# First attention in query blocks of 256, its weights 44 slots behind its maxima, and a block-float feed-forward on three PSUM banks

## The chip, the cores and the metric

One core of a Trainium2 chip runs one launch. The metric is device time in microseconds (us); less is better.

## The reference

The input is x, 2 sequences of 1024 rows of 128 floats.

```python
x = x + attn0(layernorm(x))        # 16 heads of width 8, softmax over all 1024 keys
x = x + ffn0(layernorm(x))         # fp4-quantised gate, up and down, width 352
x = x + encoder(layernorm(x))      # 6 layers: attention with a mask by i & j == 0, LN, gelu FFN of 512
x = x + relu(layernorm(x) @ W1 + b1) @ W2 + b2
```

Quantisation works on blocks of 16 values: the block's largest magnitude over 6 is the scale, each value goes to the nearest of 0, 0.5, 1, 1.5, 2, 3, 4, 6 times it. Activations are quantised before gate and up and again before down.

## The kernel before

**Two passes per attention.** A *half* is one sequence (1024 rows). A half has 4 *units*: unit k is 8 heads (k // 2) against 512 queries (k % 2). The A pass scores with queries on the partitions and takes each query's largest score: PE writes a 128x512 bank of `pA` (4 matmuls side by side on 32 columns of the array each, line 653), DVE reduces it (line 936). 64 such A steps make a unit. `dve_max` (from line 884) joins the unit's maxima, negates them, splits them into three bf16 pieces, and turns them (line 920) into the tile `mt`. SyncE (SP) moves the pieces by DMA into three rows of the stacked queries `QS` (`move_max`, line 1029), so that the B pass's matmul subtracts the maximum by itself.

The B pass scores again with keys on the partitions (line 673, 4 matmuls per 128x512 bank of `pB`), ACT takes the exponential into a ring `PB` of 10 buffers (line 798), and for every 64 keys 4 float32 matmuls of 512 columns multiply by the values and sum in the one bank `pO` (line 688: "AV" below). There are 3 banks `pA`, 2 `pB`, 1 `pO` and 2 `pG`; `pG` serves the small jobs.

**Slots.** Every engine runs the same list of slots, in order (`pe_half`, `act_half`, `dve_half`). A half of the first attention has 256 slots: slot u holds A step u, the B step that is `lead` slots behind (74), the AV whose last B step was 2 slots earlier, and then jobs by name from the table `DENSE_JOBS`, whose entries are (slot, name). Jobs are the projections of the next half (`ht`, `qk`, `split`, `v`), the output path (`oev`, `ot`, `on`, `div`, `aht`, `wo`, `res`), the LayerNorm (`gl`, `gn`) and quantisation (`gr`) in front of the feed-forward, and the feed-forward of the first sequence itself: `gx` transposes, `gg` gate and up of one tile of 128 rows (lines 1276 and following), `gs` silu on ACT, `gm` product on DVE, `gq` quantisation of two tiles on DVE, `gh` transposes, `gd` down. Every queue is in order, so a slot number says only what stands before what.

After the second half come the *drain* slots, in which no A step of the first attention is left: its last 74 B steps, and the first sequence's feed-forward. The second sequence's feed-forward runs among the slots of the second attention, whose table and steps are another path (`sparse`).

**The feed-forward's banks.** A tile's gate and up need two banks. `gate_up` (line 1143) gives the first sequence two pairs, (`pA` 0, 1) and (`pA` 2, `pG` 0), used in turn, and `turn` (line 1144) gives `gh` and `gd` bank `pG` 1. Because `pG` also serves the attention's output, `ot2`, `ot3`, `gg1`, `gg3` and `gh0` wait for each other's readers.

**SP's queue** (`sp_half`) is in order too: moves of maxima, loads of the stacked queries and keys (lines 1005, 1015) and writes of the split queries and keys (lines 1021, 1022). A unit's three moves wait for `dve_max` and for the moves before. PE's first B step of a unit waits for all three.

Of the kernel before, what the change touches and what calls it, by code (L numbers as in the profile page):

```python
# [16 lines left out]
NB = S // P  # L17
# [19 lines left out]
GRID_LOW = (0.25, 0.75, 1.25, 1.75)  # L37

# [46 lines left out]
class AStep:  # L85
# [4 lines left out]
    def __init__(self, k, parts, second, tiles, groups):  # L90
        self.k, self.parts, self.second, self.tiles, self.groups = k, parts, second, tiles, groups
        self.width = parts[0][4]


class BStep:


    def __init__(self, k, parts):
        self.k, self.parts = k, parts
        self.cols = sum(p[3] for p in parts)  # L100


def a_steps(sparse):
    out = []
    for k in range(UNITS):
        x = k % 2
        if not sparse:
            for r in range(NR):
                for gg in range(2):
                    for half in range(2):  # L110
                        out.append(AStep(k, [(gg, x * NR + r, ("half", half), 0, CH)], half, (r,), (gg,)))
            continue
# [33 lines left out]
def b_steps(sparse):  # L146
# [3 lines left out]
    for k in range(UNITS):  # L150
        x = k % 2
        if not sparse:
            sets = [(kt,) for kt in range(NK)]
            pop = dict.fromkeys(range(NK), 0)
        else:
            kts = range(NK) if x == 0 else range(NK // 2)
            pop = {kt: ones_in(kt & 7) for kt in kts}
            sets = [(kt,) for kt in sorted(kts, key=lambda kt: pop[kt]) if pop[kt] < 3]
            sets.append(tuple(kt for kt in kts if pop[kt] == 3))
# [29 lines left out]
class Attn:  # L189
# [3 lines left out]
    def __init__(self, sem, tag, sparse, halves):  # L193
# [3 lines left out]
        self.period, self.lead = (82, 36) if sparse else (256, 74)  # L197
        self.jobs = SPARSE_JOBS if sparse else DENSE_JOBS
        self.end = max(at - (halves - self.owned(name)) * self.period
                       for t in self.jobs.values() for at, name in t) + 1  # L200
        self.a_end = [max(i for i, st in enumerate(self.a) if st.k == k) for k in range(UNITS)]
# [90 lines left out]

    def a_bank(self, half, n):
# [5 lines left out]
    def ring(self, n):  # L299
# [5 lines left out]
PBUF = 10  # L305
ABANKS, BBANKS, OBANKS = 3, 2, 1
# [1346 lines left out]
```

## Time and profile before

| | before |
|---|---|
| runs, us | 1934.43, 1927.29, 1935.47; median 1934.43 |
| the profiled execution, time / span, us | 1923.19 / 1921.4 |
| PE, DVE, ACT busy share | 85%, 73%, 63% |
| mean granted TensorE clock | 0.941 of 2.4 GHz |
| first A step | 44.3 us |
| first B step | 108.2 us |
| last A step's reduction of the first attention ends | 454.7 us |
| last AV of the first attention ends | 528 us |
| first A step of the second attention | 594.6 us |

All times inside the span are microseconds from its start. Busy time of PE is modelled and overlaps itself; the distance between the starts of neighbouring rows tells more. "Idle before <- X" names what ended an engine's wait.

### The profile page before, as it was taken

The page shows a single profiled execution, that of the slowest core. Times are in us where ns is not written, and L with a number is a line of the kernel's source. Part 1 is how long each engine was busy: PE and PEld are TensorE (multiplying, and loading weights), DVE is VectorE, ACT ScalarE, POOL GpSimd, SP SyncE. Part 2 cuts the span into 40 slices and gives each one's busy share as a digit, 9 for nine tenths or more (in the row PEclk, how much of TensorE's full clock was granted, in tenths as well). Part 3 has the DMA queues.
Part 4 walks back from the last instruction along what each step waited for, and adds up shares of the span by engine and source line. Part 5 has one row for each costly group of instructions (what it writes and reads, how often), then busy time and mean ns, then how long its engine had stood idle before and what let it go on. Part 6 is the DMA issues. An engine that isn't in the chain of part 4 may idle for free.

```text
span 1921.4 us, 67094 instructions
## 1 busy us (share of the span) xinstructions
PE 1634.4 (85%) x28905; PEld 909.1 (47%) x28905; DVE 1406.8 (73%) x3351; ACT 1200.9 (63%) x2142; POOL 258.9 (13%) x239
## 2 busy tenths in 40 slices
PE   3899998999856788888989888888889897988896
PEld 1233333233333455655556565555555555655553
DVE  7888888886768767675767768576757676876755
ACT  2157776677831567676766767666766776776652
POOL 2000000000011112020302121121202120301111
PEclk7579999999977899999999999999999999999998
DMA  7022102001031532434242433333333424253000
GB/s 175 1 51 80 39 3 51 3 3 27 5 97 39 142 65 73 100 90 97 54 120 53 129 72 94 74 105 64 79 94 77 111 63 111 53 135 65 7 7 17
DMA packets 153756, 130.83 MB, mean 68 GB/s; under 512 B 65029, under 2 KB 149445, under 8 KB 151445
## 3 DMA queue, kind: packets, MB, share of 16 engines
q1 hardware_dynamic: 136181, 125.75, 26.7%
q8 instruction: 228, 3.74, 0.8%
q10 hardware_dynamic: 17280, 0.79, 0.6%
q14 instruction: 67, 0.55, 0.1%
HBM read 79.25 MB, written 45.88 MB: 65 GB/s over the span
## 4 chain that ended last, share of the span: by engine, by line
PE 39%; DVE 10%; ACT 8%; issue 5%; DMA 4%; ACTq 1%; POOL 0%; SPq 0%; POOLq 0%; DVEq 0%
PE pB L673 8%; PE pO L688 7%; PE pA L653 6%; PE pG L622 5%; PE pG L632 5%; DMA emr<-sce 4%; DVE mx L936 3%; ACT PB L798 3%; PE pG L567 2%; ACT VD L756 2%; ACT HT L711 1%; PE pG L599 1%; DVE bst L475 1%; PE pG L581 1%; PE pG L586 1%
## 5 line engine op out<-in xcount | busy, mean ns | idle before, releaser
L798 ACT ACTIVATE PB<-pB 128x512 f32<-128x512 f32 (+1 forms) x1496 | 838.7, 593 | 436.1 <-PE pB L673 409.5
L936 DVE TENSOR_REDUCE mx<-pA 128x1 f32<-128x512 f32 (+3 forms) x1000 | 635.9, 669 | 114.0 <-PE pA L653 112.8
L673 PE MATMUL pB<-QS,KS 85*32 85x256 bf16 (+3 forms) x11264 | 599.9, 284 | 67.2 <-ACT PB L798 45.1
L653 PE MATMUL pA<-KS,QS 82*32 82x256 bf16 (+2 forms) x8384 | 541.3, 311 | 85.1 <-DVE mx L936 40.1
L688 PE MATMUL pO<-PB,VD 128*32 128x128 f32 (+3 forms) x5632 | 459.0, 399 | 6.7 <-issue 4.9
L673 PEld LDWEIGHTS pB<-QS,KS 85*32 85x32 bf16 x11264 | 261.7, 97 | 342.5 <-ACT PB L798 237.4
L653 PEld LDWEIGHTS pA<-KS,QS 82*32 82x32 bf16 x8384 | 203.8, 97 | 310.2 <-DVE mx L936 112.4
L936 DVE TENSOR_REDUCE mxb<-pA 128x1 f32<-128x512 f32 x304 | 207.0, 681 | 11.0 <-PE pA L653 10.8
L498 POOL TENSOR_TENSOR rstd<-vareps,mhalf 128x4 f32<-128x4 f32 x68 | 69.1, 1017 | 1057.8 <-DVE vareps L484 1056.8
L688 PEld LDWEIGHTS pO<-PB,VD 128*32 128x32 f32 x5632 | 160.3, 111 | 34.7 <-issue 7.5
L622 PE MATMUL pG<-HT,wL 128*128 128x512 f32 x192 | 96.0, 624 | 27.7 <-ACT HT L711 25.2
L840 DVE TENSOR_TENSOR ON<-pG,em 128x288 f32<-128x288 f32 x48 | 20.7, 452 | 120.1 <-ACT em L737 120.0
L632 PE MATMUL pG<-wL,FF 128*128 128x128 f32 x768 | 91.8, 278 | 3.5 <-ACT FF L732 3.5
L632 PEld LDWEIGHTS pG<-wL,FF 128*128 128x128 f32 x768 | 87.5, 192 | 9.5 <-ACT FF L732 9.5
L982 POOL TENSOR_TENSOR VU<-VN 128x512 f32<-128x512 f32 x12 | 15.3, 1276 | 517.8 <-PE pG L586 517.8
L732 ACT ACTIVATE FF<-pG,cL 128x512 f32<-128x512 f32 x96 | 66.0, 687 | 21.2 <-PE pG L622 19.3
L849 DVE TENSOR_TENSOR ON<-ON,pG 128x288 f32<-128x288 f32 x48 | 21.6, 452 | 78.0 <-PE pG L599 77.2
L567 PE MATMUL pG<-HT,wE 128*128 128x512 f32 x112 | 68.7, 705 | 9.0 <-ACT HT L711 8.7
L622 PEld LDWEIGHTS pG<-HT,wL 128*128 128x128 f32 x192 | 33.0, 191 | 76.5 <-issue 45.2
L510 PE MATMUL pG<-ident,N 128*128 128x128 f32 x320 | 54.1, 293 | 16.9 <-DVE N L491 14.7
L491 DVE TENSOR_SCALAR N<-N,mv,rstd 128x128 f32<-128x128 f32 x208 | 57.9, 342 | 12.7 <-POOL rstd L498 12.7
L756 ACT ACTIVATE VD<-VN 64x256 f32<-64x256 f32 x112 | 48.5, 433 | 21.6 <-DVE VN L834 16.0
(186 smaller groups left out, 1526.9 us busy)
## 6 DMA issues: line engine op xcount, KB each, us to landing
scq<-PQ SPq DMA_DIRECT2D x84, 384.0 KB, 3.5
QS<-scq SPq DMA_DIRECT2D x56, 576.0 KB
KS<-sck SPq DMA_DIRECT2D x84, 384.0 KB
sck<-PK SPq DMA_DIRECT2D x28, 384.0 KB, 5.4
wL<-in_wL SPq DMA_DIRECT2D x6, 576.0 KB, 4.7
QS<-mt SPq DMA_DIRECT2D x168, 8.0 KB, 2.1
rE<-in_rE SPq DMA_DIRECT2D x7, 256.0 KB, 12.1
emr<-sce SPq DMA_DIRECT2D x96, 4.0 KB, 1.7
```

The costliest lines, as they stand in the source:

```text
L491: ins = v.tensor_scalar(dst[:, t, :], src[:, t, :], mv[:, t, 0:1], rstd[:, t:t + 1], ALU.subtract, ALU.mult)
L498: g.tensor_tensor(rstd[:, a], vareps[:, a], mhalf[:, a], ALU.pow).then_inc(ln.rs, 1)
L567: pe.matmul(pG[:, bank, :], wE[:, n[1], :], HT[:, c * CH:(c + 1) * CH], start=True, stop=True)\
L622: pe.matmul(pG[:, bank, :], wL[:, D + n[1] * P:D + (n[1] + 1) * P], HT[:, c * CH:(c + 1) * CH], start=True, stop=True).then_inc(F1.filled, 1)
L632: ins = pe.matmul(pG[:, bank, i * P:(i + 1) * P], FF[:, x, k, i * P:(i + 1) * P], wL[:, D + HID + k * D:D + HID + (k + 1) * D], start=(k = ...
L653: ins = pe.matmul(pA[QT * hd:QT * (hd + 1), a.a_bank(half, n), at:at + width], QS[0:R_A, r // NR, head, r % NR * QT:(r % NR + 1) * QT], ro ...
L673: ins = pe.matmul(pB[32 * i:32 * (i + 1), a.b_bank(h, v), at:at + width], KS[0:R_B, head, k0:k0 + 32], allowed(QS[0:R_B, x, head, :], 3, k ...
L688: ins = pe.matmul(allowed(pO[32 * j:32 * j + 32, k % OBANKS, :], 3, kt & 7 if a.sparse else 0), VD[:, col:col + 32], PB[:, a.ring(bank)[0] ...
L732: act.activation(FF[:, x, m, :], pG[:, a.bank[name], :], ACT.Gelu, bias=cL[:, 2 + m:3 + m])\
L756: ins = act.activation(VDv[KT * ab:KT * (ab + 1), half.b, 2 * TC * x + p:2 * TC * (x + 1):2, :, VW * ab:VW * ab + HD], src[:, :, :, ab, :] ...
L798: act.activation(PB[:, pos_, 0:st.cols], pB[:, a.b_bank(h, v), 0:st.cols], ACT.Exp).then_inc(a.b_exped, 1)
L936: v.tensor_reduce(dst[:, gs[0]:gs[-1] + 1, tl[0]:tl[-1] + 1:step], pA[:, a.a_bank(half, n), 0:len(gs) * len(tl) * st.width] .rearrange("p ...
```

## The change

Six things change together, all in the first attention and the first sequence's feed-forward.

1. A unit's queries fall into two blocks (`sub`) of 256. A B step now holds two pairs of heads times 256 queries in its bank in place of one pair times 512: 8 matmuls of 256 columns in place of 4 of 512. Its exponential is still one of 128x512. A unit still has 64 B steps: 32 for block 0, then 32 for block 1.
2. An AV stands behind every second B step and is 4 matmuls of 256 columns; before, behind every fourth, and of 512.
3. `dve_max` runs after 32 A steps, on 16 of the 32 columns; its three transposes (line 920) are as before.
4. `QS` is laid out by block (`QD`), a stack of queries is loaded by two DMAs, and a block's maxima are moved by 12 DMAs (3 pieces times 4 pairs of heads, 16 partitions of 32 values each) in place of a unit's 3 (128 partitions of 32).
5. `lead` is 44 in place of 74.
6. The first sequence's feed-forward has one gate and up pair (`pA` 0, 1) and turns in `pA` 2, so it no longer touches `pG`; the waits between `pG`'s users go, and `DENSE_JOBS` is a new table. POOL clears `mp` once at the start.

```diff
-        self.period, self.lead = (82, 36) if sparse else (256, 74)
+        self.period, self.lead = (82, 36) if sparse else (256, 44)
...
+            for sub in range(SUBS):
+                for kt in range(NK):
+                    parts = []
+                    for j0 in range(0, NJ, SUBS):
+                        bank = [(kt, j0 + i, i * SQ, SQ) for i in range(SUBS)]
+                        parts += [(kt, j, len(steps), o, w) for kt, j, o, w in bank]
+                        steps.append(BStep(k, bank, sub))
+                    bundles.append((k, len(steps) - 1, parts))
...
-                    if n == a.a_end[st.k]:
-                        dve_max(v, a, half, st.k)
+                    if n == a.a_end[st.k][st.sub]:
+                        dve_max(v, a, half, st.k, st.sub)
...
-            sp.dma_start(QS[0:R_PAIR, x, hs, :], q[:, hs, x * CH:(x + 1) * CH])\
-                .then_inc((a.stack, a.stack_x1)[x][s], 16)
+            for u in range(SUBS):
+                at = x * CH + u * SQ
+                sp.dma_start(QD[0:R_PAIR, x, u, hs, :], q[:, hs, at:at + SQ]).then_inc(there, 16)
...
+                for hd in range(NQ):
+                    p0 = QT * hd + QT // SUBS * sub
+                    head = SH * s + 2 * hd
+                    sp.dma_start(QD[R_A + i:R_A + i + 1, x, sub, head:head + 2, :].rearrange("p h t -> p (h t)"),
+                                 mt[p0:p0 + QT // SUBS, x, i, :]).then_inc(a.m_loaded, 16)
...
-        gate_up = [[(pA[:, 0, :], pA[:, 1, :]), (pA[:, 2, :], pG[:, 0, :])], [(pB[:, 0, :], pB[:, 1, :])]]
-        turn = [pG[:, 1, :], pO[:, 0, :]]
+        gate_up = [[(pA[:, 0, :], pA[:, 1, :])], [(pB[:, 0, :], pB[:, 1, :])]]
+        turn = [pA[:, 2, :], pO[:, 0, :]]
...
-                if not a.sparse and half.off == 1 and x == 2:
-                    pe.wait_ge(gu_done, 2)
-                if not a.sparse and half.off == 1 and x == 3:
-                    pe.wait_ge(gu_done, FT)
-                    pe.wait_ge(dn_added, FU)
...
-                elif b == 0 and n == 1:
-                    pe.wait_ge(A0.ot_read, UNITS + 1)
-                if b == 0 and n == 3:
-                    pe.wait_ge(A0.res, CB + 1)
...
-                if b == 0 and n == 0:
-                    pe.wait_ge(A0.aht_ready, CB + 1)
```

The table of jobs moves names between slots. Its ACT part in the drain (slots counted from the first half's start, so that 512 is the first drain slot):

```diff
-    "act": [(9, "gw0"), (512, "gx0"), (513, "gx1"), (515, "gs0"), (515, "gs1"), (269, "oev2"), (272, "on2"), (276, "aht0"),
-          (539, "gs2"), (539, "gs3"), (541, "gh0"), (545, "gh1"), (547, "gs4"), (-219, "ht0"), (549, "gs5"),
+    "act": [(512, "gx0"), (512, "gx1"), (9, "gw0"), (522, "gs0"), (534, "gs1"), (534, "gs2"), (537, "gs3"),
+          (540, "gh0"), (541, "gh1"), (541, "gs4"), (545, "gs5"), (548, "gh2"), (548, "gs6"), (549, "gh3"),
```

What it does to the queues, at the places of which the prediction speaks. First PE in the middle of a half, where A and B steps alternate (A is `pA`, B is `pB`, AV is `pO`). Before:

```order
L688 MATMUL pO<-PB,VD 32x512 x4
L653 MATMUL pA<-KS,QS 32x512 x4
L673 MATMUL pB<-QS,KS 32x512 x4
L653 MATMUL pA<-KS,QS 32x512 x4
L673 MATMUL pB<-QS,KS 32x512 x4
L653 MATMUL pA<-KS,QS 32x512 x4
L673 MATMUL pB<-QS,KS 32x512 x4
L653 MATMUL pA<-KS,QS 32x512 x4
L673 MATMUL pB<-QS,KS 32x512 x4
L688 MATMUL pO<-PB,VD 32x512 x4
```

Changed:

```order
L712 MATMUL pO<-PB,VD 32x256 x4
L675 MATMUL pA<-KS,QS 32x512 x4
L695 MATMUL pB<-QS,KS 32x256 x8
L675 MATMUL pA<-KS,QS 32x512 x4
L695 MATMUL pB<-QS,KS 32x256 x8
L712 MATMUL pO<-PB,VD 32x256 x4
```

Half an AV stands after two slots where a whole one stood after four.

Then SP from the first stack loads on. Before:

```order
L1015 DMA KS<-sck 24x8192 x3
L1005 DMA QS<-scq 72x8x512
L1029 DMA QS<-mt 1x128x32 x3
L1005 DMA QS<-scq 72x8x512
L1015 DMA KS<-sck 24x8192 x3
```

Changed:

```order
L1055 DMA KS<-sck 24x8192 x3
L1046 DMA QS<-scq 72x8x256 x2
L1088 DMA QS<-mt 1x16x32 x24
L1046 DMA QS<-scq 72x8x256 x2
L1055 DMA KS<-sck 24x8192 x3
```

The 24 moves are 12 for each block of a unit; the rest of the order is the same.

Last ACT in the drain, from the feed-forward's transposed input (`HT<-pA`) on; `PB<-pB` is a B step's exponential, the other `pA` rows are silu. Before:

```order
L1310 ACTIVATE HT<-pA 128x512
L798 ACTIVATE PB<-pB 128x512 x2
L1316 ACT_TABLE_LOAD
L1316 ACTIVATE FF<-pA 128x352
L1316 ACTIVATE x<-pA 128x352
L798 ACT_TABLE_LOAD
L798 ACTIVATE PB<-pB 128x512 x10
```

Changed:

```order
L1360 ACTIVATE HT<-pA 128x512 x2
L823 ACTIVATE PB<-pB 128x512 x10
L1366 ACT_TABLE_LOAD
L1366 ACTIVATE FF<-pA 128x352
L823 ACT_TABLE_LOAD
L823 ACTIVATE PB<-pB 128x512 x12
L1366 ACT_TABLE_LOAD
L1366 ACTIVATE x<-pA 128x352
L1366 ACTIVATE FF<-pA 128x352
L823 ACT_TABLE_LOAD
```

The first tile's silu stands 10 exponentials behind the transposed input, the second's another 12 behind; before, both stood 2 behind it. Between here and the first sequence's last silu there are 14 table loads in place of 10.

## Rows read from the trace of the kernel before

**Rows 1.** Windows, all engines: busy us (instructions), granted TensorE clock, DMA share, GB/s.
```profile
44.30:77.00 32.70, 32.65 (x211) 8.81 (x215) 28.46 (x47) 2.67 (x6) 0.00 (x0) 0.50 0.05 11
77.00:107.00 30.00, 22.05 (x126) 7.62 (x129) 23.50 (x45) 6.07 (x12) 0.00 (x0) 0.56 0.06 14
107.00:117.00 10.00, 9.50 (x80) 2.42 (x76) 7.04 (x11) 5.62 (x11) 0.00 (x0) 0.50 0.78 153
120.00:250.00 130.00, 125.40 (x1748) 41.03 (x1744) 111.22 (x198) 96.39 (x179) 0.00 (x0) 1.00 0.16 45
250.00:360.00 110.00, 98.80 (x1312) 34.01 (x1301) 98.51 (x196) 72.70 (x133) 2.03 (x2) 0.98 0.11 24
360.00:454.70 94.70, 91.46 (x1268) 30.08 (x1272) 80.49 (x136) 70.00 (x131) 0.00 (x0) 1.00 0.01 2
454.70:548.00 93.30, 70.98 (x608) 30.96 (x600) 60.45 (x139) 64.64 (x118) 9.45 (x9) 0.96 0.09 18
548.00:594.60 46.60, 29.93 (x102) 19.37 (x102) 33.41 (x61) 17.08 (x37) 0.00 (x0) 0.75 0.49 131
```

**Rows 2.** Windows of line 653 (maxima's scores) alone: four matmuls are one step.
```profile
44.30:77.00 32.70, 26.82 (x192) 5.23 (x196) 0.50 0.05 11
77.00:120.00 43.00, 19.96 (x160) 4.22 (x159) 0.57 0.27 56
120.00:250.00 130.00, 67.94 (x696) 18.44 (x692) 1.00 0.16 45
250.00:360.00 110.00, 50.54 (x512) 13.75 (x508) 0.98 0.11 24
360.00:454.70 94.70, 48.92 (x500) 13.37 (x500) 1.00 0.01 2
```

**Rows 3.** Timeline, a clean stretch, PE then ACT: start us, us, instruction, idle before.
```profile
201.45 0.40 PE L653 MATMUL pA<-KS,QS 82*32 82x512 bf16 x4 [0.72 <-DVE mx L936]
201.90 1.03 PE L688 MATMUL pO<-PB,VD 128*32 128x512 f32 x8
202.98 0.39 PE L673 MATMUL pB<-QS,KS 85*32 85x512 bf16 x4
...
204.78 1.03 PE L688 MATMUL pO<-PB,VD 128*32 128x512 f32 x8
...
203.42 2.19 ACT L798 ACTIVATE PB<-pB 128x512 f32<-128x512 f32 x4 [0.70 <-PE pB L673]
```

**Rows 4.** Timeline of DVE, seven reductions with nothing between.
```profile
601.99 4.34 DVE L936 TENSOR_REDUCE mx<-pA 128x1 f32<-128x512 f32 x7
```

**Rows 5.** Timeline of PE in the second attention, B steps of 256 columns.
```profile
651.28 0.39 PE L673 MATMUL pB<-QS,KS 85*32 85x256 bf16 x8
651.50 0.39 PE L653 MATMUL pA<-KS,QS 82*32 82x512 bf16 x4
```

**Rows 6.** Timeline at the end of a unit's maxima.
```profile
197.68 0.39 PE L653 MATMUL pA<-KS,QS 82*32 82x512 bf16 x4
...
200.85 1.76 SPq L1029 DMA_DIRECT2D QS<-mt  x3
```

**Rows 7.** Lines 1029 and 1043: DMA issue, ns min/median/max, and landing.
```profile
L1029 SPq DMA_DIRECT2D QS<-mt x168: 468/594/1531, 101.4 to 1817.1; - x168
...
DMA to landing us min/median/max: 1.9/2.1/10.4
...
L1043 SPq DMA_DIRECT2D emr<-sce x96: 303/432/1997, 620.6 to 1790.3; - x96
```

**Rows 8.** Groups of ACT, 454.7 to 528 us: count, busy, mean ns, idle before.
```profile
L798 ACT ACTIVATE PB<-pB 128x512 f32<-128x512 f32 x74 | 40.8, 600 | 9.7 <-PE pB L673 9.4
L1316 ACT ACT_TABLE_LOAD x5 | 6.4, 1283 | 0.1
```

**Rows 9.** Timeline of PE: one tile's gate and up.
```profile
461.10 1.45 PE L1276 MATMUL pA<-wF,HT 128*128 128x352 f32 x4
```

**Rows 10.** Page, groups: weight loads of line 673, count, busy, mean ns, idle.
```profile
L673 PEld LDWEIGHTS pB<-QS,KS 85*32 85x32 bf16 x11264 | 261.7, 97 | 342.5 <-ACT PB L798 237.4
```

More of the change, by code:

```diff
@@ L291, in owned, with moved @@
         return self.halves - 1
+    def moved(self, k, sub):
+        block = 16 * NP * (NQ if self.subs > 1 else 1)
+        return block * (self.subs * k + sub + 1)
     def a_bank(self, half, n):
@@ L305 @@
 PBUF = 10
+SUBS = 2
+SQ = CH // SUBS
 ABANKS, BBANKS, OBANKS = 3, 2, 1
@@ L687, in pe_half @@
                             col = ((h.b * NK + kt) * (H // 2) + NJ * (k // 2) + j) * PW
-                            ins = pe.matmul(allowed(pO[32 * j:32 * j + 32, k % OBANKS, :], 3, kt & 7 if a.sparse else 0),
+                            out, q0 = pO[32 * j:32 * j + 32, k % OBANKS, :], SQ * a.b[bank].sub
+                            ins = pe.matmul(allowed(out, 3, kt & 7) if a.sparse else out[:, q0:q0 + SQ],
                                             VD[:, col:col + 32], PB[:, a.ring(bank)[0], at:at + width],
-                                            start=(kt == 0), stop=(i + 1 == a.av_end[k]), tile_position=(0, 32 * j),
+                                            start=(kt == 0), stop=(i + 1 == a.av_end[k] or not a.sparse and kt == NK - 1),
+                                            tile_position=(0, 32 * j),
                                             skip_group_check=True)
@@ L882, in dve_job, with dve_max @@
                 ln_norm(v, ln2, N, N, c, half, ln_in)
-        def dve_max(v, a, half, k):
-            x, kb = k % 2, k % 2
-            m, e = mx[:, kb, :], emx[:, kb, :]
+        def dve_max(v, a, half, k, sub):
+            x, kb, z = k % 2, k % 2, a.subs * k + sub
+            cols = slice(sub * MC // a.subs, (sub + 1) * MC // a.subs)
+            m, e = mx[:, kb, cols], emx[:, kb, :]
+            hi, mid, lo = (mp[:, i, cols] for i in range(NP))
+            res = mres[:, cols]
             def mxw(i):
-                half.wait(v, a.mx, MXN * k + i, MXN * UNITS)
-            half.wait(v, a.a_reduced, a.a_end[k] + 1, a.na)
+                half.wait(v, a.mx, MXN * z + i, a.nmx)
+            half.wait(v, a.a_reduced, a.a_end[k][sub] + 1, a.na)
             if a.sparse:
@@ L931, in dve_half @@
                     if n == a.a_first[st.k]:
-                        half.wait(v, a.mx, MXN * (st.k - 1), MXN * UNITS)
+                        half.wait(v, a.mx, MXN * a.subs * (st.k - 1), a.nmx)
                     gs, tl = st.groups, st.tiles
                     step = tl[1] - tl[0] if len(tl) > 1 else 1
-                    dst = (mxb if st.second else mx)[:, kb, :].rearrange("p (g r) -> p g r", g=2)
+                    dst = (mxb if st.second else mx)[:, kb, st.sub * MC // a.subs:(st.sub + 1) * MC // a.subs]\
+                        .rearrange("p (g r) -> p g r", g=2)
+                    tl = [r % (NR // a.subs) for r in tl]
                     v.tensor_reduce(dst[:, gs[0]:gs[-1] + 1, tl[0]:tl[-1] + 1:step],
@@ L1024, in move_max @@
         def move_max(sp, a, half, k):
[L1025 to L1030 removed]
+            for sub in range(a.subs):
+                move_rows(sp, a, half, k, sub)
             if a.sparse and k < UNITS // 2:
```

93 lines of the change are left out of this document (60 added, 33 removed), and 34 rows, old and new, of the table DENSE_JOBS.

## The prediction

> **What bounds the kernel now.** I read the windows by stage first. The first attention with its fill and drain takes the span up to 548 us; the 46.6 us after it [rows 1] and the 1327 us from 594.6 us to the end hold no line whose instructions or order change, so the time must move before 548 us. Line 653's own windows turn stages into slots [rows 2]: 48 steps by 77 us and 40 more by 120 us (12 of these with B steps), 174 to 250 us, 128 to 360 us, 125 to 454.7 us. That is 0.75 us a slot in the two clean stretches (299 slots in 224.7 us) and 0.86 us in the middle, where the first sequence's LayerNorm and quantisation keep DVE at 98.5 of 110 us [rows 1].
>
> The timeline shows what a clean slot waits for [rows 3]. AV starts at 201.90 and again at 204.78: 2.88 us for four slots. The work between is 8 A and B steps, 0.22 us apart, and one AV of 0.86 us (202.76 less 201.90, the row before 202.98 by 0.22): 2.60 us. The missing 0.28 us are PE's waits for ACT: while PE spends 0.86 us in one AV, ACT runs dry (it was idle 0.70 us before 203.42), and then two `pB` banks are too few to catch up at 0.55 us an exponential. PE is the bound, but its work comes in lumps. At a unit's end a second wait stands: DVE is away in `dve_max`, and PE stood 0.72 us for it at 201.45. DVE needs 0.60 us a slot (seven reductions in 4.34 us, the last still running 0.68) [rows 4].
>
> The drain from 454.7 to 548 us is a third case: DVE is busy 60.5 of 93.3 us, ACT 64.6, PE 71 [rows 1], and each waits for the others in the chain gate and up, silu, product, quantisation.
>
> **The steady slots: AV in halves.** Two slots now hold 4 steps of 0.22 and half an AV, 0.43: 1.30 us. One bank's loop is score to exponential 0.44 us (202.98 to 203.42), exponential 0.60, back to PE 0.05: 1.09 us for two banks, and two exponentials take 1.10. Both fit into 1.30, so ACT's wait goes: 0.65 in place of 0.72 us a slot, -0.07. Against it, `dve_max` comes twice as often. Of the 3.2 us from a unit's last A step at 197.68 to the first move at 200.85 [rows 6] some 1.4 are the score, a short queue and the 0.68 us reduction; the other 1.7 to 1.8 are `dve_max`, five small operations and three transposes, which I cost the same at half the width; with 0.60 + 1.7/32 = 0.65 us a slot DVE is now as full as PE, and the 0.7 us wait comes once in 32 slots in place of 64: +0.015. Net -0.055 us over 299 clean slots is -16 us. In the 128 crowded slots DVE rules, and I take -3 us. Together **-19 us**. Ends: nothing gained, or all of 0.75 - 0.65 over the 299 slots, -30 us.
>
> Does a matmul of 256 columns cost half of one of 512? The second attention has them: eight of 256 at 651.28, and the next group starts at 651.50 [rows 5], 0.22 us like four of 512. I cost the doubled count at nothing; it is hidden because four column groups of the array run side by side. The Trainium skill speaks against this: "TensorE: Matmul & The Clock Gate", section "Back-to-back issue gap", gives a stream of weight load and matmul pairs some 81 ns a matmul at 128 columns and 131 ns at 512. By a straight line between those two figures, an estimate, eight pairs of 256 would take 0.76 us against 0.52 for four of 512. The measured 0.22 decides, since those groups run the very same shape.
>
> **The moves of maxima.** Before, three moves were issued in 1.76 us from 200.85 [rows 6], 3.2 us after the unit's last A step started at 197.68, and landed 2.1 us after issue [rows 7]; 3.2 + 2 x 0.59 + 2.1 = 6.5 us, against 11 slots of 0.72 and the wait, 8.9. So there was room, and no B step waits for them to speak of. Now 12 stand in SP's queue: 3.2 + 11d + 2.1 us. PE reaches the B step after 13 slots of 0.65, one step and the 0.7 to 1.0 us wait for DVE: 9.7 us. The deadline is met for d up to 0.40 us. No row shows a move of 16 partitions. The nearest are the old move, 0.594 us with 128 partitions, and line 1043's with 32 partitions, 0.432 us, and 0.303 at least [rows 7]. I take 0.43, from the row nearest in size: arrival at 10.0 us, PE waits 0.3 us a block. Of the 13 blocks between 120 us and the last A step 9 lie in clean slots: **+3 us**. Ends: 0.30 us, no wait; 0.594, arrival at 11.8 and 2.1 us a block, +19 us and about +2 in the crowded ones. Behind a waiting PE stand A steps too, so nothing hides this.
>
> The Q stacks' second DMAs add about 0.3 us of issue before the first A step; the clearing of `mp` on POOL is done long before DVE asks for it. I count both as nothing.
>
> **The fill.** B steps now start at slot 44, about 74.5 us, not at 108.2. The 42 slots up to 120 us took 45.5 us with 12 B steps; now all carry one. At full clock PE needs 42 x 0.65 = 27 us and some 5 for the projections. The clock was at 1.2 GHz in nearly all of 44 to 107 us and still for 10 us after the B steps came, with PE busy 9.5 of 10 us, and at 2.4 GHz from then on [rows 1]. If it rises again 10 us after PE fills up, that adds 5 us: 37 us. DVE needs 42 x 0.60, 7 for splits, 1 for values, 1.7 for `dve_max`: 35. Both fit into 45.5 us, but they wait for each other and for ACT. I take **+2 us**. Ends: -5 us; and +19 us if the clock stays low throughout (42 x 1.30 + 10 = 65 us).
>
> **The drain.** 30 of 74 B steps leave it, 16.4 us of ACT at 0.548 us. They were cover, not bound: ACT had 40.8 us of exponentials and 10 table loads of 1.28 us [rows 8]. What bounds the drain next is the chain through DVE, whose 60.5 us of work stay. New idle time stands at its head: the first tile's silu comes behind 10 exponentials (5.5 us), gate and up of 1.45 us [rows 9] and a table load; the second behind 12 more with two loads. DVE has 4.6 us of other work before the first and 0.5 between, so it idles some 14 us. One pair of banks in place of two sets each tile's gate and up behind the tile before; from the third tile on DVE has 3 to 4 us of quantising between two products, enough for 1.45 + 0.5 us and mostly for the four added table loads (5.1 us on ACT). I leave 10 us for this, for the second sequence's output path (`aht1`, `wo1`), and the last down product. 60.5 + 14 + 10 = 84.5 against 93.3: **-9 us**. What it gives up are waits for `pG` and the tail from the last AV at 528 us to 548 us, when the second sequence's path ran alone; with B steps done about 50 us after the last A step it runs beside quantisation. Ends: -19 us (no idle but the head's) and +5 us.
>
> **Sum.** -19 + 3 + 2 - 9 = -23 us. The profiled execution took 1923.2 us (span 1921.4 and 1.8 around it); it would be 1900. The median of the runs, 1934.4, lies 11.2 us above it, and I carry the difference over: **1911 us**.
>
> **Rivals.**
> *The moves come late* (slower). Place: PE's first B step of each block; SP's queue decides, not PE. Each 0.1 us of d above 0.43 costs 1.1 us a block, about 14 us in 13 blocks. The gain is gone at d near 0.6; from 0.70 us on the change is slower by over 0.5%. At 0.75 us: 9 x 3.85 + 4 x 2.3 = 44 us, so -19 + 44 + 2 - 9 = +18, **1952 us**. For it: the one row of this very kind of move is 0.594, its maximum 1.5. Against: every transfer with fewer partitions is cheaper to issue. Chance 0.13.
> *The ends give nothing back.* The one pair of banks makes the drain as long as before less 2 us, and the fill pays 12 us at low clock: -19 + 3 + 12 - 2 = -6, **1928 us**. For it: ACT, PE and DVE wait in turn, in order, and the table loads grow. Against: the 33 us that DVE idles in the old drain. Chance 0.25.
> *Short matmuls cost more.* If the weight loads of line 673 did not hide, each 97 ns on average [rows 10], four more a slot would be 0.39 us over 468 slots, +182 us: **about 2090 us**. Nothing in [rows 5] shows it. Chance 0.02. (It is the mechanism that the Trainium skill's rule above would have.)
> The forecast keeps 0.60.
>
> **Numbers.** A measurement of this kernel tells about 0.5%, 9.7 us, from no change. Faster by more (under 1924.8): the forecast's 0.60 and 0.07 of the second rival, 0.67. Within 0.5%: the rest of the second rival and 0.01 of slow moves, 0.19. Slower: 0.12 and 0.02, 0.14. Range: downward steady slots at -27, drain at -16 and no wait for moves give 1892; upward the old move's 0.594 us (+18) alone gives 1929, with part of the fill's low clock 1940. I give 1891 to 1940.
>
> **What the next profile shows if this is right.** AV rows 1.30 to 1.35 us apart and PE's waits for `PB` nearly gone; 0.69 us a slot between 120 us and the last A step, which ends near 441 us; 12 issues of about 0.43 us, and waits of PE for `QS<-mt` of a few tenths; the clock at 2.4 GHz from about 85 us; DVE's last quantisation in front of the second attention's projections about 85 us after the last A step. It is wrong if PE waits over 1 us a block for the moves, if the clean slots stay above 0.72 us, or if the drain lasts 93 us again.

## The result, and the profile after

| us | before | after |
|---|---|---|
| median of the runs on this chip | 1930.86 (4 runs, 1923.33 to 1935.47) | 1968.51 (4 runs, 1946.25 to 1979.82) |
| ratio | | 1.0119, interval 1.0065 to 1.0173 |
| the profiled execution, time / span | 1923.19 / 1921.4 | 1946.25 / 1944.5 |
| mean granted clock | 0.941 | 0.933 |
| first A step | 44.3 | 46.2 |
| last A step's reduction ends | 454.7 | 484.5 |
| first A step of the second attention | 594.6 | 616.7 |

The change is slower, by 1.2% (0.7 to 1.7); 1911 us was forecast. The ratio leaves out the two executions of the change that took over 1.5% longer than its quickest, so it is smaller than the quotient of the medians (1.0195). The profiled execution is the quickest of the four. The two profiled executions differ by 23.1 us: +1.8 up to the first A step, +28 from there to the last reduction (438.3 in place of 410.4), -7.7 from there to the second attention (132.2 in place of 139.9), +1.0 after it. So the whole loss lies in fill and steady slots, where I had expected a gain of 14.

The waits of PE between 40 and 520 us, longest in total first (total, times, longest):

```profile
PE pB L695 <- DMA QS<-mt: 24.6, 12, 2.6
PE pA L675 <- DMA KS<-sck: 20.7, 1, 20.7
PE pA L675 <- DVE mx L971: 10.1, 14, 1.5
PE pA L675 <- DVE mxb L971: 7.4, 6, 2.6
PE pB L695 <- ACT PB L823: 7.1, 11, 1.6
```

The first of them is new: the first B step of a block (line 695, formerly 673) waits for the moves of its maxima, 2.05 us on average, in 12 blocks. This is the change's timeline at such a place, first PE from the block's last A step on, then the last two operations of `dve_max` and SP:

```profile
230.29 0.40 PE L675 MATMUL pA<-KS,QS 82*32 82x512 bf16 x4
...
238.80 0.39 PE L695 MATMUL pB<-QS,KS 85*32 85x256 bf16 x8
239.24 0.39 PE L695 MATMUL pB<-QS,KS 85*32 85x256 bf16 x8
...
239.89 0.39 PE L675 MATMUL pA<-KS,QS 82*32 82x512 bf16 x4
242.40 0.40 PE L695 MATMUL pB<-QS,KS 85*32 85x256 bf16 x8 [2.12 <-DMA QS<-mt]
...
232.53 0.17 DVE L944 TENSOR_TENSOR mp<-mres,mp 128x16 bf16<-128x16 f32 x1
232.74 0.40 DVE L953 STREAM_TRANSPOSE mt<-mp 128x32 bf16<-128x32 bf16 x3
...
233.16 8.03 SPq L1088 DMA_DIRECT2D QS<-mt  x12
```

SP issues twelve moves one behind another in 8.03 us, 0.67 us each, starting 0.02 us after the transposes end. The last lands at 242.4, 12.1 us after the block's last A step started at 230.29 (10.0 were forecast). PE had come at 240.28, 10.0 us after it (9.7 forecast). Over the steady slots an issue of 16 partitions took as long as the old one of 128 [rows 7]:

```profile
L1088 SPq DMA_DIRECT2D QS<-mt x159: 502/589/1992, 100.7 to 459.6; - x159
...
DMA to landing us min/median/max: 1.6/1.8/3.3
```

The windows by stage, in the columns of [rows 1]:

```profile
44.00:77.00 33.00, 29.33 (x191) 7.68 (x191) 28.78 (x53) 2.07 (x5) 0.00 (x0) 0.50 0.10 19
77.00:120.00 43.00, 40.55 (x740) 22.70 (x742) 36.92 (x68) 32.10 (x61) 0.00 (x0) 0.92 0.18 38
120.00:250.00 130.00, 113.72 (x2532) 72.73 (x2524) 105.55 (x198) 88.69 (x163) 0.00 (x0) 0.95 0.21 52
250.00:360.00 110.00, 95.63 (x1928) 58.67 (x1924) 95.13 (x198) 68.04 (x124) 2.03 (x2) 0.89 0.12 24
360.00:460.00 100.00, 88.80 (x1936) 56.02 (x1932) 82.82 (x156) 67.49 (x124) 0.00 (x0) 0.93 0.02 3
```

From 120 to 460 us PE is idle for 42 of 340 us (19 before), and the granted clock, 0.98 to 1.00 before, is 0.89 to 0.95. Five windows of 5 us around the wait that ends at 190.15 show how the two hang together:

```profile
180.00:185.00 5.00, 4.34 (x108) 2.75 (x104) 4.86 (x14) 3.58 (x7) 0.00 (x0) 1.00 0.03 6
185.00:190.00 5.00, 3.26 (x76) 1.82 (x68) 3.98 (x7) 2.85 (x6) 0.00 (x0) 1.00 0.03 5
190.00:195.00 5.00, 4.85 (x56) 2.53 (x60) 1.41 (x3) 2.17 (x4) 0.00 (x0) 0.51 0.00 0
195.00:200.00 5.00, 5.00 (x108) 3.06 (x104) 3.76 (x6) 3.25 (x7) 0.00 (x0) 0.81 0.01 3
200.00:205.00 5.00, 5.00 (x128) 3.56 (x121) 4.88 (x9) 4.09 (x8) 0.00 (x0) 1.00 0.02 5
```

PE stands 1.89 us (until 190.15), and then runs at 1.2 GHz for the next window and part of the one behind it (means 0.51 and 0.81): 56 matmuls in 5 us that otherwise hold 128. The clock fell in this way behind five of the nine waits for moves of about 1.9 us or more between 120 and 460 us, those that end at 163.0, 190.2, 294.5, 388.3 and 415.4:

```profile
163.00:169.60 6.60, 6.59 (x88) 3.61 (x92) 3.15 (x5) 2.98 (x5) 0.00 (x0) 0.50 1.03 338
190.20:196.80 6.60, 6.60 (x76) 3.40 (x80) 2.19 (x4) 2.77 (x5) 0.00 (x0) 0.50 0.00 0
296.00:302.60 6.60, 6.38 (x76) 3.11 (x68) 3.46 (x5) 3.77 (x7) 0.00 (x0) 0.50 0.01 2
388.20:394.80 6.60, 6.54 (x88) 3.71 (x92) 3.09 (x5) 2.98 (x5) 0.00 (x0) 0.50 0.01 2
415.50:422.10 6.60, 6.60 (x76) 3.38 (x80) 2.21 (x4) 2.77 (x5) 0.00 (x0) 0.50 0.01 2
```

Not every wait does it: after the 2.12 us at 242.40 the clock stayed at 1.00. Where no such wait stands the halves of AV do what was forecast: in a clean stretch (205.19, 206.50, 207.81) AV starts are 1.31 us apart, which is 0.655 us a slot.

My theory after reading: the moves come too late because SP needs 0.6 us for each, and a standing PE loses clock besides. Rivals: the new drain or its job order costs time in the steady part; the short matmuls and halves pay less than thought; only the waits count.

### The profile page after: what moved, and what is told of

It is laid out like the page before. It is cut to its first block, busy times and chain, and to the rows that moved or that the text cites. A ratio compares the mean times of both kernels' runs of the same rounds, so it can differ in the third digit from the quotient of the medians.

```text
span 1944.5 us, 73514 instructions
## 1 busy us (share of the span) xinstructions
PE 1630.8 (84%) x31977; PEld 1017.2 (52%) x31977; DVE 1421.7 (73%) x3415; ACT 1209.0 (62%) x2146; POOL 259.1 (13%) x240
## 4 chain that ended last, share of the span: by engine, by line
PE 40%; DVE 10%; ACT 8%; issue 5%; DMA 4%; ACTq 1%; POOL 0%; POOLq 0%; DVEq 0%
PE pB L695 8%; PE pO L712 7%; PE pA L675 6%; PE pG L637 5%; PE pG L647 5%; DMA emr<-sce 4%; ACT PB L823 3%; DVE mx L971 3%; PE pG L587 2%; ACT VD L781 2%; ACT HT L736 1%; PE pG L614 1%; DVE bst L495 1%; PE pG L601 1%; PE pG L606 1%
## 5 line engine op out<-in xcount | busy, mean ns | idle before, releaser
L695 PE MATMUL pB<-QS,KS 85*32 85x256 bf16 (+3 forms) x13312 | 611.6, 268 | 86.4 <-ACT PB L823 48.9
L675 PE MATMUL pA<-KS,QS 82*32 82x256 bf16 (+2 forms) x8384 | 547.8, 312 | 84.0 <-DVE mx L971 43.9
L712 PE MATMUL pO<-PB,VD 128*32 128x256 f32 (+3 forms) x6656 | 490.4, 367 | 9.2 <-issue 6.4
L695 PEld LDWEIGHTS pB<-QS,KS 85*32 85x32 bf16 x13312 | 319.1, 98 | 311.5 <-ACT PB L823 123.4
L712 PEld LDWEIGHTS pO<-PB,VD 128*32 128x32 f32 x6656 | 192.8, 112 | 26.6 <-issue 9.5
L637 PE MATMUL pG<-HT,wL 128*128 128x512 f32 x192 | 97.0, 630 | 27.7 <-ACT HT L736 25.2
L647 PEld LDWEIGHTS pG<-wL,FF 128*128 128x128 f32 x768 | 87.5, 192 | 9.4 <-ACT FF L757 9.4
L530 PEld LDWEIGHTS pG<-ident,N 128*128 128x128 f32 x320 | 36.6, 148 | 49.3 <-issue 21.6
```

The costliest lines, as they stand in the source:

```text
L530: ins = pe.transpose(pG[:, bank, i * P:(i + 1) * P], src[:, TC * c + i, :], ident[:, :])
L637: pe.matmul(pG[:, bank, :], wL[:, D + n[1] * P:D + (n[1] + 1) * P], HT[:, c * CH:(c + 1) * CH], start=True, stop=True).then_inc(F1.filled, 1)
L647: ins = pe.matmul(pG[:, bank, i * P:(i + 1) * P], FF[:, x, k, i * P:(i + 1) * P], wL[:, D + HID + k * D:D + HID + (k + 1) * D], start=(k = ...
L675: ins = pe.matmul(pA[QT * hd:QT * (hd + 1), a.a_bank(half, n), at:at + width], query_tile(a, r, head), row[:, keys * CH:(keys + 1) * CH] i ...
L695: ins = pe.matmul(pB[32 * i:32 * (i + 1), a.b_bank(h, v), at:at + width], KS[0:R_B, head, k0:k0 + 32], allowed(QS[0:R_B, x, head, :], 3, k ...
L712: ins = pe.matmul(allowed(out, 3, kt & 7) if a.sparse else out[:, q0:q0 + SQ], VD[:, col:col + 32], PB[:, a.ring(bank)[0], at:at + width], ...
```

## The experiments

Ten kernels ran, two of them twice, each beside the kernel before, whose medians there were 1925.6 to 1927.6 us. "Steady" below is the distance from the first A step to the start of the last reduction, "drain" from there to the second attention's first A step; both come from the one profiled execution. Before: 409.7 and 140.6. After: 437.6 and 132.9.

### Three moves a block

The maxima of the two blocks stand in alternate columns of `mx`, so the transposes put a block's maxima on every second partition, and one DMA per piece moves them.

```diff
-            cols = slice(sub * MC // a.subs, (sub + 1) * MC // a.subs)
+            cols = slice(sub, MC, a.subs)
...
-                for hd in range(NQ):
-                    p0 = QT * hd + QT // SUBS * sub
-                    head = SH * s + 2 * hd
-                    sp.dma_start(QD[R_A + i:R_A + i + 1, x, sub, head:head + 2, :].rearrange("p h t -> p (h t)"),
-                                 mt[p0:p0 + QT // SUBS, x, i, :]).then_inc(a.m_loaded, 16)
+                sp.dma_start(QD[R_A + i:R_A + i + 1, x, sub, SH * s:SH * (s + 1), :].rearrange("p h t -> p (h t)"),
+                             mt[sub::SUBS, x, i, :]).then_inc(a.m_loaded, 16)
```

(The reductions write to the same alternate columns, and the semaphore's count per block is smaller.) Expected: 

> The changed kernel, but the maxima of the two blocks stand in alternate columns, so that a block goes out in 3 moves of 64 partitions in place of 12 of 16; nothing else differs. Theory (the moves come late, and PE's stall also brings its clock down): 3 issues of 0.59 us, arrival at 3.2 + 1.2 + 2.1 = 6.5 us against the deadline of 9.7; PE's waits for QS<-mt fall from some 2 us a block to under 0.3, the clock stays at 2.4 GHz between 120 us and the last A step, which ends near 445 us and not at 484; about 1905 us. Rival 1 (only the waits count, the clock falls for another reason): waits gone, 25 us gained, about 1921, windows still at 0.89 to 0.95. Rival 2 (halves of AV and short matmuls do not pay): no more than 5 us gained, above 1940.

Measured: 1906.63 us median of 4 (1900.45 to 1921.16), ratio to before 0.9891 (0.9831 to 0.9952). Steady 405.4, drain 130.4. PE's waits in 40 to 520 us:

```profile
PE pA L675 <- DMA KS<-sck: 23.3, 1, 23.3
PE pB L695 <- ACT PB L823: 11.6, 14, 2.0
PE pA L675 <- DVE mx L970: 10.6, 15, 1.5
PE pA L675 <- DVE mxb L970: 6.7, 5, 2.6
```

and its issues of moves in the steady slots:

```profile
L1084 SPq DMA_DIRECT2D QS<-mt x42: 468/597/1469, 103.0 to 429.2; - x42
```

What follows: the waits for `QS<-mt` are gone, and with them 32.2 us of the steady part (27.7 in this kernel's second profile, further down), against 24.6 us that PE had waited. The median is 62 us under the change's; from profile to profile, where the change's execution was its quickest, 35 us. The clock is back at 1.00 from 120 to 250 us and from 360 us on, but not between 250 and 360 us (0.89). An issue still takes 0.6 us; only their number has changed. The moves made the change slow, and it is now faster than the kernel before. Most of that gain lies in the drain, 10.2 us shorter than before; the steady part is shorter by 4.3 us.

### Six moves a block

Against the version with three moves (the semaphore's count changes with it):

```diff
-                sp.dma_start(QD[R_A + i:R_A + i + 1, x, sub, SH * s:SH * (s + 1), :].rearrange("p h t -> p (h t)"),
-                             mt[sub::SUBS, x, i, :]).then_inc(a.m_loaded, 16)
+                for g in range(2):
+                    head = SH * s + 4 * g
+                    sp.dma_start(QD[R_A + i:R_A + i + 1, x, sub, head:head + 4, :].rearrange("p h t -> p (h t)"),
+                                 mt[64 * g + sub:64 * (g + 1):SUBS, x, i, :]).then_inc(a.m_loaded, 16)
```

Expected: 

> moves3 with 6 moves a block (32 partitions each) in place of 3. By issues of 0.59 us whatever their size, the last lands at 3.2 + 6 x 0.59 + 2.1 = 8.8 us against the 9.7 us at which PE comes: no waits for QS<-mt to speak of, steady part as in moves3, about 1900 to 1915 us. If an issue's price grew with small partitions, waits of about 1 us a block would show, and 1920 us.

Measured: 1912.47 us median of 8, ratio 0.9929 (0.9897 to 0.9961). Steady 396.2. No wait for `QS<-mt` stands among PE's. What follows: twice as many issues cost nothing while they fit before the deadline. The price begins at a threshold, it is no slope from the first move on.

### The moves alone, in the kernel before

The kernel before, whose unit's three moves are cut into twelve by pairs of heads; lead 74, one block a unit. The second attention keeps its three.

```diff
             for i in range(NP):
...
-                sp.dma_start(QS[R_A + i:R_A + i + 1, x, SH * s:SH * (s + 1), :].rearrange("p h t -> p (h t)"),
-                             mt[:, x, i, :]).then_inc(a.m_loaded, 16)
+                for hd in range(NQ):
+                    head = SH * s + 2 * hd
+                    sp.dma_start(QS[R_A + i:R_A + i + 1, x, head:head + 2, :].rearrange("p h t -> p (h t)"),
+                                 mt[QT * hd:QT * (hd + 1), x, i, :]).then_inc(a.m_loaded, 16)
```

Expected: 

> The kernel before, but each unit's 3 moves of maxima in 12 of 32 partitions (512 columns each a head pair); lead 74, one block a unit, drain as before. Theory: 12 x 0.59 us of issue puts arrival at 11.8 to 12.0 us against 8.9 of room, so PE waits some 3 us at each of 7 units, and the clock falls behind each: +21 us of waits and some 15 of clock, 1955 to 1970 us. Rival 1 (waits alone): +21, 1945 to 1952. Rival 2 (an issue costs less with fewer partitions, as I forecast, 0.43): +7 at most, under 1942.

Measured: 1959.37 us median of 4 (1958.38 to 1960.36), ratio 1.0158 (1.0134 to 1.0183). The wait and the issues of line 1036:

```profile
PE pB L674 <- DMA QS<-mt: 21.2, 7, 3.4
...
L1036 SPq DMA_DIRECT2D QS<-mt x84: 502/591/1619, 105.9 to 447.7; - x84
```

and its windows:

```profile
120.00:250.00 130.00, 120.31 (x1608) 38.85 (x1604) 101.70 (x176) 88.54 (x164) 0.00 (x0) 0.95 0.22 56
250.00:360.00 110.00, 95.62 (x1196) 32.76 (x1188) 87.40 (x174) 66.84 (x123) 2.02 (x2) 0.92 0.11 23
```

What follows: the model of the deadline holds on the kernel before, too. It gave 2.9 us a unit, and 21.2 / 7 = 3.0 were measured. The steady part grew by 32.4 us (442.1 less 409.7) for 21.2 us of waits, and the medians by 31.7 us. The other 11 go with the clock at 0.92 to 0.95 in place of 0.98 to 1.00: worked out from these means, an estimate, PE spent some 41 us of 120 to 460 us at 1.2 GHz in place of 4. So a late transfer cost about one and a half times its wait. The rival that only the waits count falls here; that the clock is all of the rest is the natural reading, and no kernel changes the clock alone.

### More slots between maxima and weights

The change with its twelve moves, `lead` 52 in place of 44, and the first attention's output path 8 slots later:

```diff
-        self.period, self.lead = (82, 36) if sparse else (256, 44)
+        self.period, self.lead = (82, 36) if sparse else (256, 52)
```

Expected: 

> The changed kernel with its 12 moves a block, but B steps 52 slots behind the A steps in place of 44, and the first attention's output path shifted by the same 8 slots. Theory (late moves): 8 more slots are 5.2 us more room against 2.2 us of wait, so the waits for QS<-mt go as with 3 moves and the clock stays up; 8 more B steps in the drain cost 0 to 4 us: 1900 to 1915 us. Rival 1 (only waits count): about 1922. Rival 2 (the steady slots do not pay): above 1940.

Measured: 1917.26 us median of 5, ratio 0.9935 (0.99 to 0.997). Steady 401.8, drain 139.5, no wait for `QS<-mt` in PE's list. What follows: the other remedy works as well, so at twelve DMAs it is the room that decides. It costs 7 us in the drain.

The same with three moves, leads 48 and 52. Expected, lead 48: 

> 3 moves a block as in moves3 and B steps 48 slots behind. Theory: no move wait was left with 3 moves, so more lead gives nothing in the steady part; the output path shifted by 4 slots moves DVE's div1 behind less of the quantisation; the drain holds 4 more B steps: within 6 us of moves3, 1900 to 1912. Rival (room still short, waits counted elsewhere): 10 us or more below moves3.

Expected, lead 52: 

> 3 moves a block and B steps 52 slots behind. Against lead52 (12 moves) it tells what the 12 issues still cost when PE has 5.2 us more room: theory nothing but disturbance of SP, equal to lead52 within 5 us, and its steady part equal to moves3's; drain 4 to 9 us longer than moves3's: 1908 to 1918. Rival (12 moves cost even when hidden): 10 us below lead52, near 1900.

Measured: lead 48 1907.62 us median of 10 (0.9902, 0.9866 to 0.9939), steady 403.3, drain 132.4; lead 52 1913.82 us median of 10 (0.9935, 0.9903 to 0.9968), steady 402.9, drain 139.5. Twelve or three moves at lead 52 are the same within the spread: issues that end before PE comes cost nothing to be seen. Slots beyond 48 only lengthen the drain.

### The drain alone, and one pair of banks alone

First the new drain in a kernel with one block a unit, lead 74 and three moves a unit (`SUBS` 1; the output path shifted by 30 slots, which is my own placing).

```diff
-        self.period, self.lead = (82, 36) if sparse else (256, 44)
+        self.period, self.lead = (82, 36) if sparse else (256, 74)
...
-SUBS = 2
+SUBS = 1
```

Expected: 

> The changed kernel with one block a unit, lead 74 and 3 moves a unit, so the stacks, steps and moves of the kernel before, with the new drain (one pair of banks, new job order; the first attention's output path shifted by 30 slots). It shows the drain and its table alone. Forecast of my steps: the drain from the last A step to the last quantisation some 3 to 8 us shorter, steady slots as before; 1920 to 1932 us. Rival (the new table costs time outside the drain, or one pair of banks lengthens it): above 1940 us.

Measured: 1935.71 us median of 10, ratio 1.0044 (1.0019 to 1.0069). One of the ten took 3879.9 us; it left no profile, is not in the ratio, and what happened in it stays unknown. Steady 406.1, drain 155.2, which is 14.6 us longer than before and no gain at all. So the drain's gain in the change came from the shorter lead (with the output path that moved along with it), and something in the new drain takes back more than I had allowed. The next kernel says what: the kernel before with one pair of banks for gate and up.

```diff
-        gate_up = [[(pA[:, 0, :], pA[:, 1, :]), (pA[:, 2, :], pG[:, 0, :])], [(pB[:, 0, :], pB[:, 1, :])]]
-        turn = [pG[:, 1, :], pO[:, 0, :]]
+        gate_up = [[(pA[:, 0, :], pA[:, 1, :])], [(pB[:, 0, :], pB[:, 1, :])]]
+        turn = [pA[:, 2, :], pO[:, 0, :]]
...
-         ... (557, "gg7"), (-210, "qk00"), (558, "gd1"), (-208, "qk01"), ...
+         ... (-210, "qk00"), (558, "gd1"), (559, "gg7"), (-208, "qk01"), ...
```

(`gs7` on ACT moves with `gg7`; the waits that guarded `pG` go.) Expected: 

> The kernel before with one thing of the change: gate and up of the first sequence in one pair of banks in place of two, the turn in pA's third bank (in the job order the last gate and up goes behind the second down product, which one pair demands). Forecast of my steps: each gate and up (1.45 us) waits for the product before it but is mostly hidden behind 3 to 4 us of quantising: 0 to +10 us, 1925 to 1940. Rival (the drain of one_block, 155 us from the last A step to the second attention in place of 141, comes from the one pair): about +14 us, 1940 or more.

Measured: 1944.41 us median of 4 (1943.17 to 1950.03), ratio 1.0119 (1.008 to 1.0157). Steady as before (408.5), drain 160.2. From the waits of all engines from 445 to 570 us, those of the feed-forward:

```profile
DVE FF L1339 <- ACT FF L1307: 12.7, 3, 4.9
DVE X L1363 <- PE pA L1290: 11.9, 3, 5.0
DVE FF L1339 <- ACT x L1307: 10.4, 4, 4.0
PE pA L1267 <- DVE FF L1339: 9.3, 5, 2.6
```

What follows: with one pair, gate and up (line 1267) wait 9.3 us for the products, and DVE's products (line 1339) 23.1 us for silu; in the same window of the kernel before these were 5.0 and 11.5 us. One pair of banks costs 19.6 us of drain at lead 74 (the medians differ by 17.5). I had kept 10 us for it together with other things.

Last, the change with three moves and the old two pairs; as `pG` then holds gate and up, the last output tile has to stand behind the last down product.

```diff
-         ... (306, "ot3"), ... (309, "aht1"), ... (311, "wo1"), ...
+         ... (313, "ot3"), ... (315, "aht1"), ... (317, "wo1"), ...
```

Expected: 

> moves3 with the old banks of the fp4 drain: two pairs for gate and up, the turn in pG; the last output tile (ot3, aht1, wo1 with what belongs to them) then has to stand behind the last down product, and the second attention's first use of pG waits for it. old_one_pair showed one pair at +18 us in the old drain. Theory A (a pair is dear wherever B steps and quantising don't cover it): from the last A step to the second attention 118 to 125 us in place of moves3's 130; 1895 to 1900 us. Theory B (with the B steps gone earlier the pair is nearly free, and the output tile behind it costs what it gives): within 5 us of moves3 or up to 10 us slower.

Measured: 1912.25 us median of 8, ratio 0.9915 (0.9884 to 0.9945); drain 136.2, against 128.8 to 132.9 of the kernels with three moves, lead 44 and one pair. Two pairs give nothing at lead 44, as theory B had it. Whether they save nothing there, or the output tile behind the last down product takes what they save, this kernel doesn't tell.

### An order of jobs in the crowded stretch

In `moves3` PE waited for the second output tile's division, which stood on DVE behind a quantisation; then each engine waited for the other, and the clock fell. (The 2.8 us of the expectation below are another wait of this kind, in the drain at 511.66; the one here is 2.29 us.) PE's rows at this place:

```profile
287.54 0.66 PE L530 MATMUL pG<-ident,N 128*128 128x128 f32 x4 [2.29 <-DVE N L880]
...
301.84 0.62 PE L675 MATMUL pA<-KS,QS 82*32 82x512 bf16 x4 [2.56 <-DVE mxb L970]
```

and the windows before and behind:

```profile
270.00:290.00 20.00, 16.47 (x356) 10.11 (x348) 18.24 (x34) 12.81 (x25) 0.00 (x0) 0.95 0.02 3
290.00:310.00 20.00, 16.78 (x244) 9.32 (x236) 16.11 (x42) 8.48 (x16) 1.01 (x1) 0.67 0.06 16
```

```diff
-          ... (307, "gr00"), (307, "div1"), (-202, "split01"), (311, "res1"), (312, "gl1"), ...
+          ... (307, "div1"), (308, "gr00"), (-202, "split01"), (312, "res1"), (312, "gl1"), ...
```

Expected: 

> moves3 with one change in the job order: the second output tile's division (div1) stands ahead of the quantisation gr00 on DVE, not behind it. In moves3 PE waited 2.8 us for the division, DVE then 2.6 us for PE's projection, and the clock fell to 0.5 for 10 us (290 to 315 us). Theory (a stall of 2 to 3 us also costs its clock): both waits and the fall go, the stretch from 250 to 360 us gains 4 to 8 us: 1898 to 1904 us. Rival (clock falls there for want of work in general, since DVE rules): the fall moves elsewhere in the stretch, under 2 us gained.

Measured: 1909.03 us median of 10 (1899.91 to 1920.77), ratio 0.993 (0.9901 to 0.9959). The profiled execution was the quickest, 1899.91: steady 395.4, drain 128.8. In it PE's wait for the division is 0.6 us (0.6 in place of 2.8 in the drain, too), the longest for a reduction 1.5, and the windows read

```profile
270.00:290.00 20.00, 17.43 (x368) 10.69 (x360) 17.96 (x38) 13.72 (x26) 0.15 (x1) 1.00 0.01 3
290.00:310.00 20.00, 16.53 (x304) 9.34 (x308) 18.16 (x39) 10.33 (x18) 0.86 (x1) 0.83 0.32 71
```

As the medians did not differ, both kernels ran once more, side by side. Expected, three moves again: 

> moves3 again, for a closer median beside m3_div in the same call: 1900 to 1910 us. Its profile shows whether the wait of 2.8 us for div1 and the fall of the clock at 290 to 315 us are there in each execution (theory: the wait is in the order, so yes).

Expected, the order again: 

> m3_div again beside moves3. Theory: the job order's wait is worth 4 to 8 us, so the median lies 4 to 8 us below moves3_again's. Rival (the clock falls for another stall of 2 to 3 us in other executions, and the gain of the one profile was chance): medians equal within 3 us.

Measured: 1914.07 us median of 12 (1895.43 to 1927.27) without the order (steady 409.9, drain 132.9), 1907.08 median of 6 (1895.87 to 1911.94) with it (steady 397.2, drain 128.8); ratios 0.9927 (0.9893 to 0.996) and 0.9891 (0.9851 to 0.9931). The wait for the division was there again in each profile of the old order at these slots (2.29 us in both of `moves3`, 2.28 with six moves); with the new it was 0.6 both times. But the fall of the clock did not go with it: the second profile of the new order, whose longest wait there is 1.54 us, reads

```profile
290.00:310.00 20.00, 16.44 (x256) 8.62 (x260) 17.42 (x43) 8.98 (x17) 1.01 (x1) 0.66 0.27 60
```

and six moves in the old order had a steady part of 396.2, no longer than the new order's 395.4 and 397.2. So the theory that this wait brings the clock down is not shown, and the rival (another stall does it in other executions) stands. The medians of all 16 runs each are 1911.6 and 1907.4: 4 us, while single runs of either spread over 25 to 32 us, so whether there is a gain is not settled. The version with three moves and the new order lies 0.7 and 1.1% under the kernel before in its two measurements; `moves3` (1.1 and 0.7%) and lead 48 (1.0%) can't be told from it.

## Why the prediction was wrong

**The moves of maxima: the step that failed.** I built the right deadline and put the wrong value into it. The sum 3.2 + 11d + 2.1 was weighed against PE's coming at 9.7 us, met up to d = 0.40, and I took d = 0.43 "from the row nearest in size", the 32-partition move of line 1043. The same line of argument had a row of the very same operation from the same tile to the same stack at 0.594 us, and put it down to its 128 partitions. Measured: 0.589 us median with 16 partitions, 0.591 with 32, 0.597 with 64. From 16 to 128 the number of partitions has no part in it. In a row of twelve it was even 0.67 us each (8.03 us), so that the last one started 0.9 us later than 11 x 0.594 had it. The first issue (2.9 us for 3.2), the landing (1.8 for 2.1) and PE's coming (10.0 for 9.7) were each off by 0.3 us the other way, and so the end of the range at d = 0.594, which gave 2.1 us a block, met the 2.05 us measured. The +21 us that I worked out for this end is 24.6. The rival "the moves come late" was the right one, and had 0.13; by its own words the gain was gone at d near 0.6. "Every transfer with fewer partitions is cheaper to issue" was the comparison of two different transfers.

**What was missing: the clock behind a wait.** I priced a wait as its own length. All but one of the dozen waits stop PE for about 2 us, and behind five of those between 120 and 460 us the granted clock fell to 1.2 GHz for nearly 7 us. In the kernel before with twelve moves 21.2 us of waits lengthened the steady part by 32.4; from the change to three moves 24.6 us went and 32.2 came back, and in other kernels of the same steady table (396.2 to 409.9 against 437.6) 28 to 41. The upper end of the range held d = 0.594, with 18 us for the moves and none for the clock.

**The steady slots.** Mechanism as forecast, size less. AV rows are 1.31 us apart (1.30 forecast), and ACT's waits within a block are gone. With three moves and the new order the stretch from 120 to 250 us holds 716 matmuls of line 675, 179 slots, 0.726 us each, and the one from 360 us on 112 slots in 81.3 us, also 0.726, against 0.747 and 0.758 before: a gain of 0.02 to 0.03, where I had 0.055. One part of what is missing can be seen: the end of a block takes 1.0 us (2.41 and 2.18 us between AV rows in place of 1.31), not 0.7. The crowded stretch gains 6 and 4 slots in 110 us in the two profiles with the new order and 3 with six moves, and lost 5 and 10 in the two of `moves3`; I had some +4. Short matmuls cost nothing in PE's pace: [rows 5] was the right row, and the rival that priced them at 182 us is excluded by PE's 0.22 us from one step to the next with eight matmuls of 256 columns. The Trainium skill ("TensorE: Matmul & The Clock Gate", section "Back-to-back issue gap") gives 81 ns a matmul at 128 columns and 131 ns at 512 for a stream of weight loads and matmuls; by a straight line between them, an estimate, eight of 256 take 0.78 us (the 0.76 of the forecast is a slip). The trace does not agree with it for this shape. PE's timeline of `moves3`, from one AV to the next:

```profile
408.53 0.61 PE L712 MATMUL pO<-PB,VD 128*32 128x256 f32 x8
408.97 0.39 PE L675 MATMUL pA<-KS,QS 82*32 82x512 bf16 x4
409.19 0.39 PE L695 MATMUL pB<-QS,KS 85*32 85x256 bf16 x8
409.41 0.39 PE L675 MATMUL pA<-KS,QS 82*32 82x512 bf16 x4
...
409.84 0.61 PE L712 MATMUL pO<-PB,VD 128*32 128x256 f32 x8
```

**The fill.** The clock rose when I said it would (after: mean 0.57 from 80 to 85 us, 1.00 from 85). The first B step came at 78.2 us (74.5 forecast). At 120 us the change stands at slot 90, in place of 88, though it began 1.8 us later: -3 us, near my lower end, where I took +2.

**The drain.** -9 forecast, -7.7 measured up to the second attention, and -5.8 up to the last quantisation, which is where the forecast ended (87.5 us in place of 93.3). The near hit is luck. I held the 30 B steps for mere cover and the single pair of banks for nearly free. At lead 74 the single pair costs 19.6 us; with it, at leads 74, 52, 48 and 44 the drain takes 155.2, 139.5, 132.4 and some 131 us. The shorter lead gives back 24 us, more than the pair takes, and the two errors cancelled. The leads' kernels also differ in where the output path stands, and the one of lead 74 has one block a unit, so the 24 us are for all of this together, and what the single pair costs at lead 44 no kernel shows.

**The forecast as a whole.** The profiled execution was to be 1900 us and was 1946: 46 us more. 42 of them lie in fill and steady slots (437.6 us, 395.7 forecast). The late moves with their clock took 28 to 41 us where 3 were forecast; the remaining 4 to 17 us are what fill and steady slots gave less than I had worked out, for the kernels of the same table without late moves have 396.2 to 409.9 us where 392.7 were forecast. The other 4 us are the later start, the drain and the time behind it. And the median lies 22 us above the profiled execution, where I had carried over 11. With three moves in place of twelve the medians, 1906.6 and 1914.1 us, lie at the 1911 forecast, but not by its sum: the profiled executions took 1911.3 and 1922.8 us where 1900 was worked out, with 405.4 and 409.9 us of fill and steady slots. Only with the new order did profiles reach it (1899.9 and 1895.9 us).

## What to carry to other kernels

When one transfer is cut into many, count issues, and price each by a row of the same line or the same pair of tiles, not by one whose size looks right: in this kernel 12 issues in a row took 7.5 to 8.6 us (once 9.6) with 16 or 32 partitions, and 3 did the same work once the layout let one pattern catch every second partition. Such a queue has a deadline and costs nothing before it (3 and 6 moves cost the same, 12 at eight more slots of lead too), so work out when the last piece lands and when its reader comes. A wait that stops PE for about 2 us or more should be priced with the clock that may go with it: here half the wait again in the kernel before, and between a tenth and two thirds in the change.

## What the runs showed of the hardware

An issue of a small DMA on SP took 0.59 to 0.60 us in the median for 16, 32, 64 and 128 partitions of 64 bytes each, and 1.8 us from issue to landing for the first three (2.1 for 128). Twelve in a row took 8.03 us, more than twelve medians: one of them took 1.16 us.

The granted clock fell to 1.2 GHz behind waits of PE of 1.9 to 3.4 us, but not behind each one of the same length, and was back after 3 to 14 us. Between 120 and 460 us it fell behind five of the nine such waits for moves in the change, and behind all six in the kernel before with twelve moves. Where it fell varied from one execution to the next at equal waits: the same two waits at 281 to 302 us went with a clock of 0.89 and 0.91 from 250 to 360 us in the two profiles of three moves, and 0.95 in that of six. It also fell without a wait of that length (0.66 from 290 to 310 us, above).

Some executions hold single stops of PE of about 3 us for which the profile names no releaser. In the second profile of `moves3`:

```profile
319.38 0.40 PE L695 MATMUL pB<-QS,KS 85*32 85x256 bf16 x8 [2.75 <-issue]
```

and then the same fall of the clock. Between 44 and 440 us there was at least one of 2.5 us or more in five of the profiled executions with two blocks (lead 48 and both leads of 52, two pairs, three moves again) and none in the other five nor in the four with one block. They stand at nearly the same places in all five, at 204 to 220 us and, but for two pairs, at 312 to 322 us. A clue lies in the DMA queues. All nine stops of 2 us or more there begin within 0.6 us of a 16 KB packet of queue 8, of the kind "instruction". Between 120 and 450 us the kernel before (first line) has 33 such packets and `moves3` (second line), with twice as many matmuls a B step, 55:

```profile
q8 instruction: 33, 0.54, 0.7%
q8 instruction: 55, 0.90, 1.2%
```

So the stops may be PE waiting for its own instructions, and the doubled count of matmuls may have this price after all. That is not shown: most such packets go with no stop, and no run changed this alone.
